# A fused token, state-space and expert block on one core: where u and the products with C are made

## What is computed

```
xz = x @ W_in;  xi, z = split(xz)
xc = silu(depthwise_conv(xi) + conv_b)
dt, Bm, Cm = split(xc @ W_x)
delta = softplus(dt @ W_dt + b_dt)
dA  = exp(delta[..., None] * A)
dBu = delta[..., None] * Bm[:, :, None, :] * xc[..., None]
h_t = dA_t * h_(t-1) + dBu_t          # scan over the tokens
y_t = einsum('bdn,bn->bd', h_t, C_t)  # product with C, sum over 16 states
out = (y + xc * D) * silu(z) @ W_out
```

## Time and profile before

| | |
|---|---|
| time, median of 3 runs (lowest to highest) | 1781.32 us (1778.06 to 1785.29) |
| time of the profiled execution | 1780.39 us |
| its span, first to last instruction | 1778.0 us |
| DVE busy | 1582.9 us, 89% |
| POOL busy | 1569.1 us, 88% |
| PE busy | 1475.8 us, 83% |
| ACT busy | 1329.4 us, 75% |
| mean granted TensorE clock | 0.929 |

### The profile page before, as it was taken

How to read it: one execution, slowest core, us unless ns; L and a number is a source line. 1 busy time by engine, 2 the same in 40 slices (tenths; PEclk the granted TensorE clock), 3 DMA queues, 4 the chain that set the end, 5 groups by cost and what they waited for, 6 DMA issues and landing times.

```text
span 1778.0 us, 27104 instructions
## 1 busy us (share of the span) xinstructions
PE 1475.8 (83%) x9464; PEld 1039.4 (58%) x9464; DVE 1582.9 (89%) x1387; ACT 1329.4 (75%) x3100; POOL 1569.1 (88%) x782
## 2 busy tenths in 40 slices
PE   7768888888887888888988888888888888887588
PEld 6545656555655656556666655666565656554355
DVE  2589999999999999999999999999999999999935
ACT  2577788787887888787777878878787888786644
POOL 1689999999999999999999999999998999998804
PEclk9888999998999999999998989999998999996899
DMA  3767755555666555656575555666655555656110
GB/s 112 149 129 190 155 128 114 122 120 131 136 131 141 127 125 116 127 121 146 120 152 122 119 114 125 136 135 132 141 128 117 117 126 127 137 117 137 35 34 15
DMA packets 194138, 217.94 MB, mean 123 GB/s; under 512 B 93979, under 2 KB 184485, under 8 KB 193490
## 3 DMA queue, kind: packets, MB, share of 16 engines
q1 hardware_dynamic: 193234, 215.04, 55.1%
q0 software_dynamic: 576, 1.17, 0.3%
q10 hardware_dynamic: 192, 0.01, 0.0%
HBM read 169.92 MB, written 46.62 MB: 122 GB/s over the span
## 4 chain that ended last, share of the span: by engine, by line
POOL 30%; DVE 30%; issue 15%; ACT 12%; PE 11%; DMA 2%; SPq 1%; DVEq 0%; ACTq 0%; POOLq 0%
POOL xr L1629 18%; DVE psum L1302 12%; DVE xr L1302 12%; POOL xr L1637 10%; ACT psum L1005 4%; DVE xr L1311 2%; PE psum L789 2%; DVE vv L1373 2%; PE psum L613 2%; PE psum L790 2%; ACT soft L1053 1%; ACT soft L1057 1%; PE psum L704 1%; ACT soft L1061 1%; ACT L1127 1%
## 5 line engine op out<-in xcount | busy, mean ns | idle before, releaser
L1629 POOL TENSOR_TENSOR xr<-u,bbc 128x912 f32<-128x912 f32 x512 | 1078.9, 2137 | 15.0 <-DMA u<-u_scratch 15.0
L1005 ACT ACTIVATE psum<-delta,a_neg 128x228 f32<-128x228 f32 x2048 | 805.6, 440 | 216.4 <-DVE xr L1311 184.8
L1302 DVE TENSOR_TENSOR_SCAN psum<-psum,xr 128x912 f32<-128x912 f32 x320 | 655.8, 2049 | 66.3 <-ACT psum L1005 54.6
L1637 POOL TENSOR_TENSOR xr<-xr,cbc 128x912 f32<-128x912 f32 x192 | 408.5, 2128 | 35.4 <-DVE xr L1302 32.5
L1302 DVE TENSOR_TENSOR_SCAN xr<-psum,xr 128x912 f32<-128x912 f32 x192 | 392.1, 2042 | 0.0
L718 PE MATMUL psum<-xr,fold 128*32 128x228 f32 x4096 | 299.2, 390 | 85.4 <-POOL xr L1637 59.0
L1311 DVE TENSOR_TENSOR xr<-psum,cbc 128x912 f32<-128x912 f32 x320 | 353.6, 1105 | 11.5 <-DVE psum L1302 0.5
L613 PE MATMUL psum<-xh,win 128*128 128x228 f32 x1024 | 227.6, 372 | 64.1 <-ACT xs L1036 33.5
L613 PEld LDWEIGHTS psum<-xh,win 128*128 128x128 f32 x1024 | 195.6, 196 | 95.8 <-ACT xs L1036 44.2
L718 PEld LDWEIGHTS psum<-xr,fold 128*32 128x32 f32 x4096 | 97.4, 113 | 222.3 <-issue 85.7
L668 PE MATMUL psum<-xi,conv_d 128*128 128x228 f32 x1024 | 210.9, 358 | 0.0
(11 more groups left out here) (201 smaller groups left out, 1656.3 us busy)
## 6 DMA issues: line engine op xcount, KB each, us to landing
delta<-delta_scratch SPq DMA_DIRECT2D x256, 228.0 KB, 6.4
u<-u_scratch SPq DMA_DIRECT2D x256, 228.0 KB, 4.2
bbc<-bc_scratch SPq DMA_DIRECT2D x128, 114.0 KB, 2.5
u_scratch<-u SPq DMA_DIRECT2D x64, 228.0 KB, 4.8
cbc<-bc_scratch SPq DMA_DIRECT2D x128, 114.0 KB, 2.7
delta_scratch<-delta SPq DMA_DIRECT2D x64, 226.0 KB, 5.6
out<-ob SPq DMA_DIRECT2D x32, 228.0 KB
h_scratch<-h SPq DMA_DIRECT2D x31, 228.0 KB
```

What stands on the lines that cost most here:

```text
L1005: ins = nc.scalar.activation(slot(k)[:, j * TOK:(j + 1) * TOK], delta4[:, c // 2, j, c % 2], ACT.Exp, scale=a_neg[:, c, j, n:n + 1])
L1302: nc.vector.tensor_tensor_scan(x if k in ON_POOL else slot(k), slot(k), x, 0.0, ALU.mult, ALU.add).then_inc(scan_done, 1)
L1629: nc.gpsimd.tensor_tensor(xr[:, k % XRING], u4[:, c // 2, :, c % 2], bbc[:, p, n].unsqueeze(1).to_broadcast([P, J, TOK]), ALU.mult).then_i ...
L1637: nc.gpsimd.tensor_tensor(xr[:, k % XRING], xr[:, k % XRING], cbc[:, p, k % NI].unsqueeze(1).to_broadcast([P, J, TOK]), ALU.mult).then_inc ...
```

## The change

`u_out` leaves POOL and goes to DVE, right behind `delta_out`. There it waits for delta itself, for xs, and for SP's earlier stores of u. POOL's list of units changes from six to seven, none of them kept. DVE now has the products of units 1, 3, 5, 6, 8, 10, 12, 14 and 15. `ln2_moments` gets a wait of its own for the statistics, since it now comes right behind the scan s0 and before `ln2_ready` of k = 1 has been reached.

```diff
-ON_POOL = (1, 3, 8, 10, 12, 14)
+ON_POOL = (0, 2, 4, 7, 9, 11, 13)
...
+                    def u_out(g, p):
+                        dve.wait_ge(delta_done, 2 * g + 2)
+                        dve.wait_ge(xs_done, 2 * g + 2)
+                        for half in range(2):
+                            need(dve, u_out_s[half], 16 * g)
+                        nc.vector.tensor_tensor(u[:], delta[:], xs[:, p], ALU.mult).then_inc(u_done, 2)
...
                     def ln2_moments(g):
+                        dve.wait_ge(st2_done, g + 1)
...
                         image_tokens(1)
                         delta_out(0)
+                        u_out(0, 0)
...
                             if k == 7 and runs(i + 1):
                                 delta_out(i + 1)
+                                u_out(i + 1, q)
                             if runs(i):
                                 times_c(i, p, k)
...
-                    def u_out(g, p):
-                        pool.wait_ge(delta_done, 2 * g + 2)
-                        for half in range(2):
-                            need(pool, u_in[half], 16 * NQ * g)
-                        nc.gpsimd.tensor_tensor(u[:], delta[:], xs[:, p], ALU.mult).then_inc(u_done, 2)
...
-                            if k == 7 and runs(i + 1):
-                                u_out(i + 1, q)
```

## The result

The changed kernel takes 1805.19 us (median of 4 runs, 1804.31 to 1810.92), the kernel before on the same chip 1781.97 us. The ratio is 1.0143, with a 95% interval of 1.0121 to 1.0164: slower by 1.4%. The profiled execution took 1804.31 us, with a span of 1802.2 us and a mean granted clock of 0.942. The forecast was 1812.

The account below looks back on a forecast made before the run. DVE was taken as the bound, with ACT at step start and PE by way of ACT at delta. Terms +21.1, +9, +3.9, -1.0 and -1.1 made +31.9 on 1780.4: 1812 us, range 1783 to 1843.

Parts of the forecast that it names:

- the lock at u: On DVE, u with two SBUF inputs waits until POOL's running product c7 ends: 1.1 us, ends 0 and 2.1.
- the products behind their own scans: On DVE from s8 to the next s0, p8, p10, p12 and p14 directly follow their scans: 1.27 us more with p15.
- delta's wait: DVE's waits for delta, 18.2 us before, come back by half through PE's lowered clock: +9 us, ends 0 and 56.
- s0 to s2: Start of DVE's step: ACT's chain is untouched, so the distance stays at 7.65 us.
- `v_norm` and s5: DVE from s2 to s5: one product less, part lost at the lock; s5 at 16.33 instead of 17.29, 0.96 us saved.
- Delta: DVE from s5 to delta: as before, 8.19 us, so delta starts at 24.52 us behind s0.
- s8 to s0: DVE from s8 to the next s0: 22.69 us before, 1.27 us more after.
- POOL: 23 instructions a step, 48.8 us, not the bound; its wait for delta turns up as waits at c2 and c9.
- The rest: Outside the 28 steps: steps 0 to 2 cost +3.9 us, step 31 gives -1.0, the first group -1.1.
- no lock: Rival: u doesn't wait for POOL, step 50.55 us; 1769 us without delta waits (chance 0.08), 1787 with them (0.08).
- The full wait: Rival: a POOL product starts right ahead of u, which waits 2.1 us instead of 1.1; 1843 us, chance 0.10.
- the low clock in every step: Rival: the gap ahead of c2 lowers PE's clock, delta waits 2 us in all 28 steps; 1859 us, chance 0.08.

Follow-up runs that it names:

- the kernel after with `v_norm` freed: The changed kernel, with `v_norm` reading 1/sigma from PSUM where ACT writes it; u keeps two SBUF inputs: 1805.8 us, ratio 1.0155.
- The kernels with u from PSUM: The changed kernel with u reading dt in PSUM (other values): 1778.67 us; or delta written to PSUM and copied to SBUF by ACT: 1780.02 us.
- The kernels with c4: The kernel before with unit 4's product on POOL instead of unit 3's: 1838.76 us; the same with `v_norm` reading 1/sigma from PSUM: 1758.51 us.
- the kernel with u and `v_norm` both freed: The changed kernel with u on DVE from delta in PSUM, ACT copying delta to SBUF, and `v_norm` reading 1/sigma from PSUM: 1763.53 us, ratio 0.9895.
- the kernel before with `v_norm` freed: The kernel before with `v_norm` reading 1/sigma from PSUM, nothing else changed: 1742.49 us, ratio 0.9789.
- Seven products with u on POOL and `v_norm` freed: The kernel before with the change's seven units on POOL, u still there, and `v_norm` reading 1/sigma from PSUM: 1753.93 us, ratio 0.9851.
- two kernels with seven products and u on POOL: The kernel before with the change's seven units on POOL: 1893.59 us; the same with 0.4 us more on ACT ahead of `v_norm`'s input: 1893.51 us.

## Why the prediction was right

Its mechanism is what the runs show: the step was to grow from 50.19 to 51.65 us and grew to 51.61, by the lock at u and the products behind their own scans. The time came out 7 us lower, for the most part by one term, delta's wait. Point by point:

- **s0 to s2** was to stay at 7.65: 896.62 - 888.96 = 7.66. The idle was to be 2.0 and is 0.99 + 0.89.
- **`v_norm` and s5.** s5 was to come at 16.33, with 0.96 saved: it comes at 905.22 - 888.96 = 16.26. `v_norm` waits 0.47 us for ACT and 0.4 us at the lock, as the step had it (its input due at 15.3 to 15.5). In odd steps it asks 0.3 us sooner and waits 0.7 us at the lock.
- **Delta** at 24.52: 24.45. **u** 1.1 us at the lock: it asks 1.01 us behind c7's start and takes 2.07, and s8 comes at 27.61 (27.69). This was the one unknown with wide ends, 0 and 2.1, and the value in the middle held because c7 and u are both tied to s7. The margin was thin: in steps 3 to 29 POOL stood only 0.03 to 0.06 us ahead of c7, and in the kernel after with `v_norm` freed, where DVE comes there sooner than POOL, u takes 2.2 to 2.6 us. (The prediction's 27.69 is its end of c7 and 0.90, not the 1.0 that its text says; measured are 0.88.) The kernels with u from PSUM show it by itself: 51.61 - 50.64 = 0.97 a step.
- **s8 to s0**: 940.57 - 916.57 = 24.00 (23.96).
- **POOL** wasn't to pay back, and its waits were to turn up at c2 and c9: 1.32 and 1.11 us.
- **Delta's wait** is the mis-sized term. +9 us were set for waits that come back; there is one left, 2.9 us. The stretch that answers to the earlier trace rows, s2 of step 3 to s2 of step 31 (columns as there), and PE in step 15:

```profile
225.71:1673.77 1448.06, 1196.91 (x7984) 837.23 (x7980) 1366.77 (x1062) 1129.62 (x2651) 1374.01 (x645) 0.96 0.58 125
```

```profile
849.32 0.59 PE L718 MATMUL psum<-xr,fold 128*32 128x228 f32 x8 [1.61 <-POOL xr L1647]
...
853.74 0.69 PE L789 MATMUL psum<-h,plus 115*114 115x256 f32 x2 [1.57 <-DVE vv L1381]
856.50 1.77 PE L704 MATMUL psum<-dbl,wdt 17*128 17x228 f32 x8 [0.78 <-ACT ob L1117]
```

The stretch is 1448.06 - 1425.10 = 22.96 us longer: 28 x 51.61 = 1445.1 and 2.9. The gaps of PE ahead of c2 and `v_norm`, 1.61 and 1.57 us, are there as foreseen, but the projection behind them took 1.77 us, the time of full clock in the earlier trace rows, and the granted clock of the stretch is 0.96 where it was 0.94. So the step from these gaps to a lowered clock and a delta that is late by it failed. The clock still falls in 25 of the 27 steps 3 to 29, but 20.6 us behind s0 or later, when the projection is over or nearly so. Step 16, in which the projection runs from 908.1 to 909.9 (columns as in the earlier trace rows):

```profile
888.96:909.50 20.54, 17.63 (x124) 12.44 (x123) 18.15 (x17) 18.18 (x43) 19.12 (x11) 1.00 0.39 96
915.70:919.05 3.35, 3.31 (x16) 2.25 (x17) 3.32 (x3) 1.38 (x4) 3.35 (x2) 0.50 1.11 184
```

In the kernel before all of the 11 steps with a delta wait, and no other from step 3 on, have a stretch at 0.50 that begins 16.2 to 18.5 us behind s0, while the projection is due at 20.2. In six of them the projection takes 3.37 us (delta waits of 1.9 us and more), in the other five it takes 1.77 and begins 1.3 to 1.6 us late (waits of 0.8 to 1.1 us). In steps 3 to 29 of the kernel after no such stretch lies between 16.2 and 20.6 us, and the projection begins at 19.15. The one wait that is left, in step 30, comes with one that begins 14.2 us behind s0. That `v_norm` is done 1 us sooner than before doesn't explain it alone, since delta is asked for 1 us sooner too. The kernels with c4 show that `v_norm`'s lateness can bring the waits (17 against 5), and in the kernel before they fall from 18.2 to 5.8 us when `v_norm` alone is freed and PE's wait for c3 stays. The kernel after lacks that wait as well; which of the two kept the waits away here, no run parts.

- **The rest.** Steps 0 to 2 cost 2.7 us (3.9 in the sum), the end -1.9 (-1.0). The first group gave back nothing. POOL at the start:

```profile
60.37 6.25 POOL L1639 TENSOR_TENSOR xr<-u,bbc 128x912 f32<-128x912 f32 x3 [56.64 <-DMA u<-u_scratch]
```

Against 60.00 in the earlier trace rows the first product starts 0.37 us later although u was made sooner, so the 0 that the prediction gave as the other end was right, and the -1.1 taken was wrong; the first scan is 0.4 us later. Not for the reason given there, though: SP issues the first read of u at 51.40 (51.30 before), 0.7 us behind the last of the four reads of delta, and by the landings as the profile matches them that is when u's own store has landed (51.38, 51.28 before). That store was issued 0.39 us sooner, at 44.62, and took 0.5 us longer; why, no run shows. Sum: 0.4 + 2.7 + 23.0 - 1.9 = 24.2, which is 1802.2 - 1778.0.

Of the rivals, "no lock" is what the kernels with u from PSUM are. It had 50.55 for the step and 1769 to 1787 for the time; they have 50.64, 1779 and 1780. The full wait and the low clock in every step didn't come. What the prediction missed altogether is that its lock already cost the kernel before more than the change does: it saw `v_norm` at 1466 instead of 385 ns and used that as a price for u only. Freed there, the kernel gains 39 us, more than the change loses.

Why does the change not pay even unlocked? Take the kernel with u and `v_norm` both freed against the kernel before with `v_norm` freed. From s2 of step 3 to s2 of step 31 it takes 1406.2 us against 1386.2. DVE's waits in it are 80.5 against 67.4 us, and the rest 1325.7 against 1318.8, which fits two more products right behind their own scans. The largest wait that is new is the one ahead of `v_norm`, which DVE now reaches before ACT has 1/sigma:

```profile
DVE vv L1391 <- ACT psum L1119: 13.0, 29, 0.5
```

Seven products with u on POOL and `v_norm` freed take 1402.3 us for the same stretch, 16 more than the kernel before with `v_norm` freed, although DVE has a product less in each step. Here POOL is the bound. The two stretches, seven products first (POOL's busy time is the fifth):

```profile
220.04:1622.35 1402.31, 1198.03 (x7994) 851.34 (x7998) 1299.59 (x1034) 1130.34 (x2651) 1401.77 (x675) 0.94 0.58 129
221.36:1607.61 1386.25, 1192.39 (x7981) 841.20 (x7980) 1318.82 (x1061) 1130.53 (x2651) 1344.74 (x646) 0.95 0.62 131
```

POOL is busy for 1401.77 of 1402.31 us with 24 instructions a step, 2.08 us each or 50.1 us a step. DVE's own work fell by 19.2 us and its waits rose by 35. Their rows name ACT and PE (13.6 us ahead of `v_norm`, 11.6 ahead of s3, and others), but a row names only the last releaser; with POOL never standing, the steps can't be shorter while its instructions take 2.08 us each. The kernel of the change has 23 instructions on POOL, which is not full there (73.6 us idle in its stretch).

## What to carry to other kernels

A VectorE operation with both inputs in SBUF is priced by what GpSimd does at that moment, not by its own length: look at shortest and median of its line, and where they differ, let a producer write one operand to PSUM (here two lines, -2.1%) before any work is moved between the engines. Where that can't be, put it where GpSimd stands waiting for something else (u took 1.11 us there), and be wary of a GpSimd instruction that is released by the same event (c4 and c7 here). A saving ahead of such a meeting can be lost at the meeting: of 0.44 to 0.70 us saved ahead of u, 0.24 were left. And before work goes to GpSimd, look at its busy time over a stretch of steps: with seven products and u it was full, 1401.8 of 1402.3 us, and was the bound.

## What the runs showed of the hardware that I had not expected

**A held VectorE instruction can be passed by several GpSimd instructions.** In two kernels with seven products and u on POOL, `v_norm` took 9.6 to 10.1 us in every one of the 14 odd steps, while POOL began four more products of 2.1 us; where other products stood beside it, a request at 0.4 to 1.0 us behind a product's start waited for that one product alone. The longest u of the kernel after asked 2.02 us behind its product's start, missed the turn and waited for the next product too; the line of u there:

```profile
L1348 DVE TENSOR_TENSOR u<-delta,xs x32: 1108/2073/3118, 43.4 to 1639.9; 128x912 f32<-128x912 f32 x32
```

The Trainium skill, "SBUF — State Buffer", section "Who interferes with whom", says that the first to issue holds the shared ports for the whole instruction and the other blocks; taken at its word, an instruction that asked first would have had its turn ahead of the next product. The traces agree for one instruction (u of 2.07 us beside c7) and not here, where four products that came later went ahead.

**Both sides pay, unequally.** VectorE waits for the rest of the running product: `v_norm` took up to 1.97 us for work of 0.39 (with c4 in place of c3). GpSimd's next product is then held for somewhat less than the VectorE instruction's own length: 0.16 us for one of 0.39, 0.86 us for one of 1.11 (the `dbu` behind c7, 2.98 instead of 2.12 us).
